# Rounding the next input over 75 slots, and another order of the weight jobs, in a one-core attention and gated-MLP kernel

## The chip, the cores and the metric

The kernel runs on one NeuronCore of a Trainium2 chip. The metric is the device time of one execution in microseconds (us). TensorE is PE in the rows (its weight loads PEld), VectorE is DVE, ScalarE is ACT, GpSimd is POOL, and SyncE (SP) issues the DMAs.

## The reference

One layer over x (4 batch elements of 512 rows by 512), with a second input ctx of the same size:

```python
x = x + tanh(g_xattn) * xattn(layernorm(x), ctx)
x = x + tanh(g_ffn) * ffn(layernorm(x))
```

xattn normalises its input and rounds it to fp8 (e4m3) four times, once for each of four projections, because q, qx, k and v each have an input scale of their own: q and qx of 16 heads of 128, k and v of 8 groups. kx and vx come from ctx without rounding. q attends over k and v, qx over kx and vx, and the two results (4096 columns) are rounded to fp8 and projected back to 512 columns. ffn is a gated MLP of width 2048 whose weights are ternary: every matrix is divided by the mean of its absolute values, rounded and cut to -1, 0 or 1:

```python
scale = jnp.clip(jnp.mean(jnp.abs(w)), EPS, None)
wq = jnp.clip(jnp.round(w / scale), -1.0, 1.0) * scale
```

The scale of a matrix has to be known before any part of it can be made ternary. That is the only order that the mathematics asks of the jobs below.

## The kernel before, in words

The program has two phases. Phase A does all attention, phase B the output projection and the MLP, 16 tiles of 128 rows. The change touches phase A only.

Phase A is a software pipeline of 512 **slots** (NSLOT). Each engine has a program of its own that runs `for n in range(FIRST, PAST)` and writes, slot by slot, what that engine does in it. Sixteen slots make one **iteration**: one batch element with one of the eight head groups, so iteration 0 to 7 is batch element 0, and so on to iteration 31. In each slot PE computes one 128x512 tile of scores (L687), DVE takes its row maximum (L977), ACT its exponential (L1323), DVE the reciprocal of the row sum (L982), ACT the high half of the scaled result (L1334), DVE the low half (`lo`, L987), SP transposes both by DMA (L441), and PE multiplies them with v nine slots after the scores (L699). `scores(n)` waits for `lo` of slot n-4. Around this the tiles of the next iteration's projections run on PE (L654, L661), with their statistics and norms on DVE and POOL, and the transposes of heads (L674) with their scaling on ACT (L1316) and their splitting into two fp16 halves on POOL (L1573, L1579). Nothing is scheduled at run time: which slot holds what is fixed by tables of slot numbers, `X_AT`, `JOB_AT`, `SCALE_AT`, `FLAG_AT`, `WG_AT` and others.

Two kinds of extra work ride in the slots, and both are moved by the change.

**The next input** (`X_AT`). In the 128 slots of batch element b, the input of b+1 is loaded, normalised, and transposed on PE through one PSUM bank in the slots 19, 24, 35 and 51 of the 128 (`turn`, one 128-column part `kt` each). ACT scales each part four times into `xqt`, once for each of the four input scales v (`x_turned`, L1244), two in the slot of the transpose and two in the next. DVE then rounds to e4m3 (`x_quant`): 8 parts of 1024 columns, each in 5 instructions (L916, L919, L921, L923, L925), so 40 instructions, one in each of the slots 62 to 101. The parts go by scale and then by half; part 2v+half. The projections of b+1 start at slot 105 of the 128 and wait for the parts of their scale (`xq_value`). This happens three times: iterations 3 to 6 (2, 16, 16 and 6 instructions), 11 to 14 and 19 to 22, in the same pattern. DVE also takes the four maxima of ctx (L840) in slots 70 to 76; POOL spreads the result (L1489, slot 83), PE makes it whole (`c_whole`, L606, slot 84).

**The weight jobs** (`JOBS`, 128 of them besides one marker called scale). A job loads 128x512 of a weight matrix into `raw[0]` or `raw[1]`, in turns:
- a *sum* (48) adds up absolute values on ACT (L1356; the read of its accumulator has a record of its own);
- a *split* (32, for the output weights) writes an fp16 half on ACT (L1348), subtracts it on POOL (L1603), takes absolute sums of the rest on ACT (L1364), and stores the rest;
- a *tern* (48) multiplies by 1/scale and adds the rounding constant on ACT (L1361), finishes on DVE (L1013, L1014), and is stored by DMA.

`job_slots` puts the jobs at every 8/3 slots: first sums and splits mixed, three sums and two splits in turn, in slots 92 to 302; then the scale; then the 48 terns in slots 309 to 437. The job of slot n has its load issued two jobs earlier, its ACT part in slot n (tern, split) or n+2 (sum, and a split's absolute sum), its DVE or POOL part in n+1, its store in n+3. `weight_sums` (DVE, slot 303), `scale_whole` (PE, L611, slot 308) and `weight_scales` (DVE, slot 309) turn the sums into the scales. `scale_whole` writes the same single PSUM bank that the head transposes and `turn` use (`ring_tables`, list `short`), and waits until its last user's readers are through. `low_sum` and `flag_whole` do the same for a flag on whether the low halves of the output weights are zero.

## Time and profile before

| | us |
|---|---|
| median of 3 runs | 1812.07 |
| the runs | 1807.82 to 1817.33 |
| profiled execution, its own time | 1815.84 |
| its span in the trace | 1814.1 |
| busy in the span: PE, DVE, ACT, POOL | 1620.1, 1533.6, 1371.8, 1100.2 |

Busy shares are averages over stages. The 512 slots lie between 114.8 us (first L977) and about 1489 us of the span; what is before is loading and preparing, what is behind is phase B. An iteration is read here as the time from every sixteenth L977 to the next, which is how the windows below were cut. A busy engine in the rows may include short waits inside a run of matmuls.

### The profile page before, as it was taken

The page shows a single profiled execution, that of the slowest core. Times are in us where ns is not written, and L with a number is a line of the kernel's source. Part 1 is how long each engine was busy: PE and PEld are TensorE (multiplying, and loading weights), DVE is VectorE, ACT ScalarE, POOL GpSimd, SP SyncE. Part 2 cuts the span into 40 slices and gives each one's busy share as a digit, 9 for nine tenths or more (in the row PEclk, how much of TensorE's full clock was granted, in tenths as well). Part 3 has the DMA queues.
Part 4 walks back from the last instruction along what each step waited for, and adds up shares of the span by engine and source line. Part 5 has one row for each costly group of instructions (what it writes and reads, how often), then busy time and mean ns, then how long its engine had stood idle before and what let it go on. Part 6 is the DMA issues. An engine that isn't in the chain of part 4 may idle for free.

```text
span 1814.1 us, 35237 instructions
## 1 busy us (share of the span) xinstructions
PE 1620.1 (89%) x11164; PEld 1005.9 (55%) x11164; DVE 1533.6 (85%) x3391; ACT 1371.8 (76%) x3439; POOL 1100.2 (61%) x1421
## 2 busy tenths in 40 slices
PE   2368899889999999999999898999999978999997
PEld 1345555555666665666566555666666633444443
DVE  7568889999897899989887999999988876777776
ACT  6458999879989998999998788899988872222222
POOL 3677888877887777787776666777767641000000
PEclk9689999999999999999999999999999999999999
DMA  3257888779999998999897989999998896243200
GB/s 104 90 151 164 186 194 190 178 169 230 230 244 196 218 226 191 205 217 250 193 216 169 224 192 200 222 229 225 251 222 169 184 246 216 70 112 87 76 24 18
DMA packets 669596, 325.48 MB, mean 179 GB/s; under 512 B 552288, under 2 KB 595424, under 8 KB 669152
## 3 DMA queue, kind: packets, MB, share of 16 engines
q1 hardware_dynamic: 669408, 323.17, 79.2%
q8 instruction: 93, 1.52, 0.4%
q14 instruction: 95, 0.78, 0.1%
HBM read 140.61 MB, written 48.23 MB: 104 GB/s over the span
## 4 chain that ended last, share of the span: by engine, by line
PE 45%; DVE 24%; ACT 12%; issue 8%; POOL 7%; DMA 4%; SPq 0%; ACTq 0%; POOLq 0%; DVEq 0%
PE psum L699 8%; PE psum L654 8%; PE psum L687 7%; PE psum L742 6%; PE psum L717 6%; DVE pp L987 5%; DVE nmx L977 5%; PE psum L661 3%; PE psum L760 3%; ACT pp L1334 2%; DMA pt<-pp 2%; ACT psum L1323 2%; PE psum L674 2%; ACT raw L1254 2%; DVE xh L960 1%
## 5 line engine op out<-in xcount | busy, mean ns | idle before, releaser
L687 PE MATMUL psum<-qk 128*128 128x512 f16 x1536 | 422.5, 384 | 21.6 <-DVE pp L987 15.8
L699 PE MATMUL psum<-pt,vv 128*128 128x512 f16 x1536 | 399.3, 383 | 37.2 <-ACT cy L1342 22.4
L654 PE MATMUL psum<-wbt,xqt 128*128 128x256 f16 (+1 forms) x4096 | 408.7, 249 | 22.1 <-DVE xqt L904 11.4
L1323 ACT ACTIVATE psum<-psum,nmx 128x512 f32<-128x512 f32 x512 | 352.4, 688 | 69.6 <-DVE nmx L977 68.0
L654 PEld LDWEIGHTS psum<-wbt,xqt 128*128 128x128 f16 x4096 | 329.5, 99 | 136.2 <-issue 18.4
L987 DVE SCALAR_TENSOR_TENSOR pp<-psum,prs,pp 128x512 f16<-128x512 f32 x512 | 378.7, 740 | 3.3 <-ACT pp L1334 3.3
L1334 ACT ACTIVATE pp<-psum,prs 128x512 f16<-128x512 f32 x512 | 366.0, 715 | 6.2 <-DMA pt<-pp 5.9
L977 DVE TENSOR_REDUCE nmx<-psum 128x1 f32<-128x512 f32 x512 | 344.8, 674 | 28.6 <-PE psum L687 28.0
L699 PEld LDWEIGHTS psum<-pt,vv 128*128 128x128 f16 x1536 | 147.5, 98 | 234.5 <-issue 54.2
L1579 POOL TENSOR_TENSOR qk<-y,qk 128x512 f16<-128x512 f32 x192 | 231.8, 1207 | 16.0
L687 PEld LDWEIGHTS psum<-qk 128*128 128x128 f16 x1536 | 143.8, 99 | 105.4 <-DVE pp L987 24.8
L661 PE MATMUL psum<-wbt,ctxh 128*128 128x256 f16 x1536 | 193.3, 277 | 0.3 <-POOL wbt L1531 0.3
L661 PEld LDWEIGHTS psum<-wbt,ctxh 128*128 128x128 f16 x1536 | 152.5, 99 | 47.2 <-issue 2.2
L1316 ACT ACTIVATE y<-psum,hb,hw 128x512 f32<-128x512 f32 x192 | 156.7, 816 | 9.4 <-PE psum L674 9.2
L1591 POOL TENSOR_TENSOR cy<-cy,cc 128x512 f16<-128x512 bf16 x128 | 152.2, 1190 | 13.1 <-DVE cy L1001 13.1
L1329 ACT ACTIVATE prs<-psm 128x1 f32<-128x1 f32 x512 | 120.0, 234 | 51.9 <-DVE psm L982 51.3
L1664 POOL TENSOR_SCALAR frs<-fmv 128x1 f32<-128x1 f32 x16 | 3.1, 193 | 255.6 <-DVE fmv L1043 255.5
L1554 POOL TENSOR_TENSOR ars<-ast,eps 128x4 f32<-128x4 f32 x128 | 36.1, 282 | 186.1 <-DVE ast L947 185.7
L1557 POOL TENSOR_TENSOR ars<-ars,mhalf 128x4 f32<-128x4 f32 x128 | 133.7, 1044 | 10.0
L1573 POOL TENSOR_SCALAR qk<-y 128x512 f16<-128x512 f32 x192 | 120.8, 629 | 30.1 <-ACT y L1316 22.4
L1448 ACT ACTIVATE sl<-psum,am 128x512 f32<-128x512 f32 x64 | 44.0, 688 | 124.5 <-PE psum L742 124.5
L982 DVE RECIPROCAL psm<-psm 128x1 f32<-128x1 f32 x512 | 78.7, 154 | 68.1 <-ACT psum L1323 66.7
(176 smaller groups left out, 2792.3 us busy)
## 6 DMA issues: line engine op xcount, KB each, us to landing
wbt<-ws SPq DMA_DIRECT2D x192, 256.0 KB, 3.7
ws<-wbt SPq DMA_DIRECT2D x64, 256.0 KB, 4.1
catd<-cy SPq DMA_DIRECT2D x64, 256.0 KB, 3.2
raw<-in_wgu SPq DMA_DIRECT2D x64, 256.0 KB, 3.6
raw<-in_w SPq DMA_DIRECT2D x32, 384.0 KB, 3.9
wbt<-catd SPq DMA_DIRECT2D x6, 2048.0 KB, 9.8
pt<-pp SPq DMA_TRANSPOSE x512, 3.8
raw<-in_wp SPq DMA_DIRECT2D x32, 256.0 KB, 3.6
```

What stands on the lines that cost most here:

```text
L654: ins = e.matmul(bank[:, o0:o0 + c1 - c0], xv[:, v, kt * 512 + tt * 128:kt * 512 + (tt + 1) * 128], wb[i][:, h, kt, c0:c1], start=kt == 0 ...
L661: ins = e.matmul(bank[:, 256:512], ctxh[:, u, kt, ts], wkvb[i][:, w, kt, :], start=kt == 0 and k == 0, stop=kt == 3 and k == 2)
L687: ins = e.matmul(SB(n), qk[i][:, jq, u, ss], qk[i][:, jk, w, :], start=k == 0, stop=k == 2)
L699: ins = e.matmul(OB, v[:, t, u, att, :], src[:, w, t, :], start=t == 0 and k == 0, stop=t == 3 and k == 2)
L977: e.tensor_reduce(nmx[:, n % 8:n % 8 + 1], SB(n), AX, ALU.max, negate=True).then_inc(s["mx"], 1)
L987: e.scalar_tensor_tensor(pp[k][:, 1, :], SB(n), prs[:, n % 8:n % 8 + 1], pp[k][:, 0, :], ALU.mult, ALU.subtract).then_inc(s["lo"], 1)
L1316: e.activation(y32[n % 2][:], psum[:, BANK["T", n], :], ACT.Identity, bias=hb[:, vec:vec + 1], scale=hw[:, vec:vec + 1]).then_inc(s["y32"], 1)
L1323: e.activation(SB(n), SB(n), ACT.Exp, bias=nmx[:, k], accum_out=psm[:, k]).then_inc(s["exp"], 1)
L1334: e.activation(pp[n % 4][:, 0, :], SB(n), ACT.Copy, scale=prs[:, n % 8:n % 8 + 1]).then_inc(s["hi"], 1)
L1557: e.tensor_tensor(rs[:, 1, :], rs[:, 0, :], mhalf[:, 0:4], ALU.pow).then_inc(s["a_rs"], 1)
L1579: e.tensor_tensor(qk[it % 2][:, j, 1, :], y32[n % 2][:], qk[it % 2][:, j, 0, :], ALU.subtract).then_inc(s["hd_lo"], 1)
L1591: e.tensor_tensor(y.bitcast(F16), y, tmp, ALU.subtract).then_inc(s["o_q"], 1)
```

## The change

- `X_AT["quant"]`: the 40 rounding instructions lie in the slots 28 to 102 of the 128, at 28 + 1.9k, so 75 slots, about every second one. Parts are ordered by half first and scale second, so the first four parts need only the transposes of slots 19 and 24 (`xy_value(b, 2 * half_ + 1, v)`). `xq_value` is adapted to the new order: the last part of scale v is number 4+v.
- `JOBS` is ordered: all 48 sums and 8 splits (slots 92 to 230), the scale (232), 20 terns (236 to 285), 24 splits with 4 terns among them (288 to 359), 24 terns (362 to 438). With the new rounding slots (28 to 102, 156 to 230, 284 to 358) the first 20 terns lie between the second and the third rounding, and all but 8 splits lie in the third.
- `SCALE_AT` moves from 303, 308 and 309 to 218, 228 and 229; `FLAG_AT` from 306, 324 and 325 to 366, 372 and 373; `WG_AT` from 444 to 448.
- The waits for an earlier store or absolute sum of the same buffer are left out where there was none (`stored`, `summed` is None).

Counted by iteration, before and after:

| iteration | 1 | 2 | 3 | 4 | 5 | 6 | 9 | 10 | 11 | 12 | 13 | 14 | 15 | 16 | 17 | 18 | 19 | 20 | 21 | 22 | 23-27 |
|---|---|---|---|---|---|---|---|---|---|---|---|---|---|---|---|---|---|---|---|---|---|
| rounding before | 0 | 0 | 2 | 16 | 16 | 6 | 0 | 0 | 2 | 16 | 16 | 6 | 0 | 0 | 0 | 0 | 2 | 16 | 16 | 6 | 0 |
| rounding after | 3 | 8 | 8 | 9 | 8 | 4 | 3 | 8 | 8 | 9 | 8 | 4 | 0 | 0 | 3 | 8 | 8 | 9 | 8 | 4 | 0 |
| terns before | | | | | | | 0 | 0 | 0 | 0 | 0 | 0 | 0 | 0 | 0 | 0 | 4 | 6 | 6 | 6 | 26 |
| terns after | | | | | | | 0 | 0 | 0 | 0 | 0 | 2 | 6 | 6 | 6 | 1 | 0 | 1 | 1 | 3 | 22 |
| splits before | | | | | | 2 | 2 | 2 | 2 | 3 | 3 | 2 | 2 | 2 | 3 | 3 | 0 | 0 | 0 | 0 | 0 |
| splits after | | | | | | 0 | 0 | 0 | 0 | 0 | 6 | 2 | 0 | 0 | 0 | 6 | 6 | 5 | 5 | 2 | 0 |

```diff
--- before.py
+++ after.py
@@ -44,12 +44,12 @@
 STORE_W = 10
 POOL_HI = 2
 ACT_NORM = 2 * 4
-WG_AT, CAT_AT, X2_AT = (444, 490), (474, 498), 507
+WG_AT, CAT_AT, X2_AT = (448, 490), (474, 498), 507
 RAMP = -4
 OUT_AT = {"clip": 17, "field": 18, "step": 19, "add": 20, "sub": (21, 23), "store": 26}
-JOBS_FROM, TERN_FROM = 92, 309
-SCALE_AT = {"sum": 303, "whole": 308, "fac": 309}
-FLAG_AT = {"sum": 306, "whole": 324, "fac": 325}
+JOBS_FROM = 92
+SCALE_AT = {"sum": 218, "whole": 228, "fac": 229}
+FLAG_AT = {"sum": 366, "whole": 372, "fac": 373}
 X_AT = {
     "load": (1, 2, 3, 4),
     "stats": (6, 8, 9, 10),
@@ -57,7 +57,7 @@
     "norm": (13, 14, 15, 16),
     "turn": (19, 24, 35, 51),
     "ctx": (62, 63, 64, 65),
-    "quant": tuple(range(62, 102)),
+    "quant": tuple(28 + k * 19 // 10 for k in range(40)),
     "bound": (70, 72, 74, 76),
     "cxp": (82,),
     "cxs": (83,),
@@ -143,9 +143,11 @@
 
 SUMS = [("sum", "wgu", j, j) for j in range(32)] + [("sum", "wd", j, 32 + j) for j in range(16)]
 SPLITS = [("split", "wp", j, j) for j in range(32)]
-JOBS = [t for i in range(16) for t in SUMS[3 * i:3 * i + 3] + SPLITS[2 * i:2 * i + 2]]
-JOBS += [("scale", None, 0, 0)]
-JOBS += [("tern", "wgu", j, j) for j in range(32)] + [("tern", "wd", j, 32 + j) for j in range(16)]
+TERNS = [("tern", "wgu", j, j) for j in range(32)] + [("tern", "wd", j, 32 + j) for j in range(16)]
+JOBS = SUMS + SPLITS[:8] + [("scale", None, 0, 0)] + TERNS[:20]
+JOBS += [t for i in range(4) for t in SPLITS[8 + 6 * i:14 + 6 * i] + TERNS[20 + i:21 + i]] + TERNS[24:]
+
+JOB_SPANS = ((92, 231, 56), (232, 233, 1), (236, 288, 20), (288, 362, 28), (362, 442, 24))
 K0 = 6 * NG
 LAST_SPLIT = max(m for m, job in enumerate(JOBS) if job[0] == "split")
 LAST_SUM = max(m for m, job in enumerate(JOBS) if job[0] == "sum")
@@ -153,9 +155,10 @@
 
 def job_slots():
 
-    scale = JOBS.index(("scale", None, 0, 0))
-    at = {JOBS_FROM + m * 8 // 3: m for m in range(scale)}
-    at.update({TERN_FROM + (m - scale) * 8 // 3: m for m in range(scale, len(JOBS))})
+    at, m = {}, 0
+    for first, last, count in JOB_SPANS:
+        at.update({first + k * (last - first) // count: m + k for k in range(count)})
+        m += count
     at[JOBS_FROM - 4] = -1
     return at
 
@@ -240,7 +243,7 @@
 
 
 def xq_value(b, v):
-    return v + 1 if b == 0 else 4 + 8 * (b - 1) + 2 * v + 2
+    return v + 1 if b == 0 else 4 + 8 * (b - 1) + 4 + v + 1
 
 
 class Queue:
@@ -906,11 +909,11 @@
             def x_quant(b, k):
 
                 part, step = divmod(k, 5)
-                v, half_ = divmod(part, 2)
+                half_, v = divmod(part, 4)
                 src = xq[b % 2][:, v, half_ * 1024:(half_ + 1) * 1024]
                 tmp, done = xtmp[:], s["x_w"]
                 if step == 0:
-                    q.wait_ge("xy", xy_value(b, 3, v))
+                    q.wait_ge("xy", xy_value(b, 2 * half_ + 1, v))
                 q.wait_ge("x_w", ((b - 1) * 8 + part) * 4 + step)
                 if step == 0:
                     e.tensor_scalar(src, src, 448.0, -448.0, ALU.min, ALU.max).then_inc(done, 1)
@@ -1008,8 +1011,10 @@
                 f, ob = raw[i][:, 0:512], raw[i][:, 512:768].bitcast(BF16)[:, 0:512]
                 stored, summed = JB[m]
                 q.wait_ge("l_t1", JV["l_t1", m])
-                q.wait_ge(f"l_st{i}", JV[f"l_st{i}", stored])
-                q.wait_ge("l_ab", JV["l_ab", summed])
+                if stored is not None:
+                    q.wait_ge(f"l_st{i}", JV[f"l_st{i}", stored])
+                if summed is not None:
+                    q.wait_ge("l_ab", JV["l_ab", summed])
                 q.done(e.tensor_scalar(ob, f, MAGIC, 1.0, ALU.subtract, ALU.min))
                 e.tensor_scalar(ob, ob, -1.0, None, ALU.max).then_inc(s["l_t2"], 1)
 
@@ -1599,6 +1604,7 @@
                     q.wait_ge("l_hi", JV["l_hi", m])
                     if stored is not None:
                         q.wait_ge(f"l_st{i}", JV[f"l_st{i}", stored])
+                    if summed is not None:
                         q.wait_ge("l_ab", JV["l_ab", summed])
                     e.tensor_tensor(o.bitcast(F16)[:, 0:512], f, wps[:, j, :], ALU.subtract).then_inc(s["l_lo"], 1)
 
```

What the engines' programs are then: first DVE in slots 328 and 329 (iteration 20). Before (L977 is the row maximum that opens a slot, L987 `lo`, L916 and L919 rounding, L840 ctx, L1013 and L1014 a tern):

```order
L977 TENSOR_REDUCE nmx<-psum 128x1
L987 SCALAR_TENSOR_TENSOR pp2<-psum,prs,pp2 128x512
L954 BN_STATS bst1<-psum 128x6
L916 TENSOR_SCALAR xqt<-xqt 128x1024
L840 TENSOR_REDUCE cpt<-xt 128x1
L1013 TENSOR_SCALAR raw1<-raw1 128x512
L1014 TENSOR_SCALAR raw1<-raw1 128x512
L982 RECIPROCAL psm<-psm 128x1
L977 TENSOR_REDUCE nmx<-psum 128x1
L987 SCALAR_TENSOR_TENSOR pp3<-psum,prs,pp3 128x512
L937 SCALAR_TENSOR_TENSOR vv0<-psum,vv0 128x256
L919 TENSOR_SCALAR xtmp<-xqt 128x1024
```

And in the changed kernel, the same two slots whole (its line numbers are three higher from L843 on: L980 for L977, L928 for L925, which is a rounding instruction):

```order
L980 TENSOR_REDUCE nmx<-psum 128x1
L990 SCALAR_TENSOR_TENSOR pp2<-psum,prs,pp2 128x512
L957 BN_STATS bst1<-psum 128x6
L843 TENSOR_REDUCE cpt<-xt 128x1
L985 RECIPROCAL psm<-psm 128x1
L980 TENSOR_REDUCE nmx<-psum 128x1
L990 SCALAR_TENSOR_TENSOR pp3<-psum,prs,pp3 128x512
L940 SCALAR_TENSOR_TENSOR vv0<-psum,vv0 128x256
L928 TENSOR_TENSOR xqt<-xqt,xtmp 128x1024
L985 RECIPROCAL psm<-psm 128x1
```

In slot 328 three instructions are gone (one of rounding, two of a tern); slot 329 keeps one of rounding.

ACT in slots 329 and 330. Before (L1323 exponential, L1334 high half, L1361 a tern's part):

```order
L1323 ACTIVATE psum,psm<-psum,nmx 128x512
L1334 ACTIVATE pp0<-psum,prs 128x512
L1307 ACTIVATE xh1<-psum,brs1 128x128
L1308 ACTIVATE xh1<-psum,brs1 128x128
L1329 ACTIVATE prs<-psm 128x1
L1323 ACTIVATE psum,psm<-psum,nmx 128x512
L1334 ACTIVATE pp1<-psum,prs 128x512
L1316 ACTIVATE y32_0<-psum,hb,hw 128x512
L1361 ACTIVATE raw0<-raw0,magic,wsc 128x512
L1329 ACTIVATE prs<-psm 128x1
```

In the changed kernel (L1328 exponential, L1339 high half, L1353 and L1369 the two ACT parts of splits):

```order
L1328 ACTIVATE psum,psm<-psum,nmx 128x512
L1339 ACTIVATE pp0<-psum,prs 128x512
L1312 ACTIVATE xh1<-psum,brs1 128x128
L1313 ACTIVATE xh1<-psum,brs1 128x128
L1369 ACTIVATE raw0,lsum<-raw0 128x512
L1334 ACTIVATE prs<-psm 128x1
L1328 ACTIVATE psum,psm<-psum,nmx 128x512
L1339 ACTIVATE pp1<-psum,prs 128x512
L1321 ACTIVATE y32_0<-psum,hb,hw 128x512
L1353 ACTIVATE wps<-raw1 128x512
L1334 ACTIVATE prs<-psm 128x1
```

The tern's one instruction is replaced by a split's two, of two different splits here.

PE in slots 307 and 308. Before (L626 is the transpose of the next input, L611 `scale_whole`):

```order
L687 MATMUL psum<-qk1 128x512 x3
L699 MATMUL psum<-pt0,vv0 128x512 x3
L654 MATMUL psum<-wbt,xqt 128x128 x16
L626 MATMUL psum<-idf,xt 128x128 x4
L687 MATMUL psum<-qk1 128x512 x3
L661 MATMUL psum<-wbt,ctxh 128x256 x12
L611 MATMUL psum<-wsc,ones 128x2
```

In the changed kernel (L629 the transpose, L690 scores):

```order
L690 MATMUL psum<-qk1 128x512 x3
L702 MATMUL psum<-pt0,vv0 128x512 x3
L657 MATMUL psum<-wbt,xqt 128x128 x16
L629 MATMUL psum<-idf,xt 128x128 x4
L690 MATMUL psum<-qk1 128x512 x3
L664 MATMUL psum<-wbt,ctxh 128x256 x12
```

The `scale_whole` directly behind the transpose of the next input is gone from here; it stands in slot 228, which is not behind such a transpose.

## Rows read from the trace of the kernel before

**Rows 1.** The page: busy time by engine; the row maximum's group, busy us, mean ns.

```profile
PE 1620.1 (89%) x11164; PEld 1005.9 (55%) x11164; DVE 1533.6 (85%) x3391; ACT 1371.8 (76%) x3439; POOL 1100.2 (61%) x1421
...
L977 DVE TENSOR_REDUCE nmx<-psum 128x1 f32<-128x512 f32 x512 | 344.8, 674 | 28.6 <-PE psum L687 28.0
```

**Rows 2.** Windows: stretch, its us, busy us (instructions) by engine, PEclk, DMA share, GB/s.

```profile
214.90:311.80 96.90, 85.94 (x612) 56.23 (x613) 86.80 (x189) 91.71 (x243) 84.27 (x104) 0.96 0.86 190
311.80:413.40 101.60, 84.00 (x590) 53.25 (x588) 97.47 (x211) 83.45 (x221) 82.03 (x96) 0.95 0.79 186
...
537.20:578.20 41.00, 37.96 (x285) 25.22 (x284) 33.31 (x76) 40.55 (x108) 30.23 (x41) 1.00 0.89 190
578.20:659.30 81.10, 79.59 (x603) 53.88 (x602) 66.47 (x151) 77.28 (x210) 60.67 (x81) 1.00 1.02 216
659.30:748.60 89.30, 83.86 (x612) 54.80 (x610) 87.37 (x192) 77.56 (x206) 67.33 (x83) 0.98 0.99 215
...
790.20:828.40 38.20, 38.20 (x290) 25.68 (x289) 32.87 (x76) 35.69 (x101) 30.28 (x41) 1.00 1.08 232
828.40:871.00 42.60, 42.56 (x322) 28.71 (x320) 38.09 (x87) 37.38 (x102) 34.54 (x49) 1.00 1.10 241
871.00:914.70 43.70, 39.23 (x282) 25.73 (x280) 34.20 (x76) 41.26 (x108) 29.34 (x40) 0.96 0.84 191
914.70:954.50 39.80, 39.80 (x303) 26.98 (x302) 33.57 (x78) 39.22 (x106) 31.25 (x42) 1.00 1.05 219
954.50:1002.30 47.80, 44.63 (x319) 29.66 (x317) 38.20 (x87) 38.70 (x98) 30.77 (x41) 0.93 0.81 176
1002.30:1099.80 97.50, 85.35 (x602) 53.97 (x600) 95.03 (x216) 76.68 (x188) 62.19 (x78) 0.96 0.94 203
1099.80:1144.00 44.20, 39.22 (x288) 24.86 (x287) 43.99 (x97) 37.89 (x96) 31.59 (x40) 1.00 0.86 199
...
1183.70:1304.00 120.30, 118.29 (x890) 79.01 (x888) 116.86 (x259) 108.50 (x277) 87.19 (x115) 1.00 1.08 230
1342.60:1420.90 78.30, 78.30 (x594) 53.10 (x593) 66.03 (x149) 66.64 (x173) 56.00 (x77) 1.00 0.96 198
```

**Rows 3.** Timeline of PE: start, us, instruction, and in brackets its idle time before.

```profile
380.62 0.77 PE L606 MATMUL psum<-spread,ones 128*128 128x128 f32 x2 [6.66 <-POOL spread L1489]
...
969.32 0.59 PE L611 MATMUL psum<-wsc,ones 128*128 128x2 f32 x2 [3.17 <-ACT xqt L1244]
...
1016.62 1.39 PE L699 MATMUL psum<-pt,vv 128*128 128x512 f16 x3 [3.71 <-DMA pt<-pp]
...
1064.20 0.50 PE L606 MATMUL psum<-spread,ones 128*128 128x128 f32 x2 [2.74 <-POOL spread L1489]
```

**Rows 4.** A rounding group of DVE in 659.3 to 748.6 us: busy us, mean ns.

```profile
L919 DVE TENSOR_SCALAR xtmp<-xqt 128x1024 uint16<-128x1024 uint16 x7 | 6.0, 861 | 0.0
```

**Rows 5.** The tern's DVE groups in 1002.3 to 1099.8 us.

```profile
L1013 DVE TENSOR_SCALAR raw<-raw 128x512 bf16<-128x512 f32 x12 | 6.0, 503 | 0.0
...
L1014 DVE TENSOR_SCALAR raw<-raw 128x512 bf16<-128x512 bf16 x12 | 3.5, 294 | 0.4
```

**Rows 6.** The job groups of ACT, and POOL's, over the whole span.

```profile
L1361 ACT ACTIVATE raw<-raw,magic,wsc 128x512 f32<-128x512 f32 x48 | 40.6, 845 | 2.4 <-DMA raw<-in_wgu 1.3 <-DMA raw<-in_wd 1.1
L1603 POOL TENSOR_TENSOR raw<-raw,wps 128x512 f16<-128x512 f32 x32 | 38.6, 1206 | 3.0 <-ACT wps L1348 3.0
L1356 ACT ACTIVATE raw<-raw 128x512 f32<-128x512 f32 x48 | 32.3, 673 | 0.0
L1348 ACT ACTIVATE wps<-raw 128x512 f16<-128x512 f32 x32 | 21.7, 679 | 0.7 <-DMA raw<-in_wp 0.7
L1364 ACT ACTIVATE raw<-raw 128x512 f32<-128x512 f16 x32 | 21.4, 669 | 7.7 <-POOL raw L1603 7.7
```

**Rows 7.** Timeline at 714 us: a GpSimd and a VectorE instruction.

```profile
713.98 1.20 POOL L1579 TENSOR_TENSOR qk<-y,qk 128x512 f16<-128x512 f32 x1
714.10 1.36 DVE L919 TENSOR_SCALAR xtmp<-xqt 128x1024 uint16<-128x1024 uint16 x1
```

## The prediction

> **What bounds the kernel now.** The page gives PE 89%, DVE 85%, ACT 76% of the span [rows 1]. Such an average settles nothing for a change that only moves work, so I read the windows by iteration [rows 2]: which engine is full, and where. Four kinds of stretch show.
>
> - Iterations 28 and 29 (1342.6 to 1420.9) have no rounding and no job: 39.15 us each, PE busy all of it, DVE 33.0, ACT 33.3. That is the floor, set by PE. Iterations 24 to 26 add 18 terns: DVE goes to 38.95 each (97%), and the time only to 40.1.
> - Iterations 12 and 13 (659.3 to 748.6) hold 32 rounding instructions: DVE 87.4 of 89.3 us, 98%. Iterations 20 and 21 (1002.3 to 1099.8) hold as many and 12 terns: DVE 95.0 of 97.5. Iteration 22 has DVE 44.0 of 44.2. DVE sets the pace there; PE's `scores` wait for `lo`, which DVE gives late.
> - Iteration 9 (537.2 to 578.2) has ACT 40.55 of 41.0; iteration 17 ACT 41.3 of 43.7. Two transposes of the next input fall into each, eight scalings on ACT, beside mixed jobs.
> - Iterations 2 and 3 (214.9 to 311.8) have ACT 91.7 of 96.9, DVE 86.8; iterations 4 and 5 (311.8 to 413.4) DVE 97.5 of 101.6.
>
> The rounding is thus bunched in three places where DVE is full, with PE-bound iterations that leave DVE 6 us each on both sides. The timeline of PE [rows 3] shows single stalls in the same places: 6.66 and 2.74 us before `c_whole` in iterations 5 and 21, whose chain starts on the late DVE, and 3.17 us before `scale_whole` in iteration 19, where PE waits for ACT to read the transpose that lies in the same bank. The granted clock of iteration 19 is 0.93 of full [rows 2]: it fell from 2.4 to 1.2 GHz for part of the stretch, after that idle time. So a stall is paid twice.
>
> **Prices.** *Rounding instruction on DVE.* Iterations 12 and 13 have 87.37 - 2 x 33.02 = 21.3 us more than the floor [rows 2]; 2.7 us I give to the four ctx maxima, at the 0.674 us of the row maximum, a reduction of the same size [rows 1]. The rest by 32 is 0.58 us, which I take. Ends: 0.4, if nothing holds it up, and 0.86, the mean of one of the five steps there [rows 4].
> *Tern on DVE.* Where DVE is full, 0.503 + 0.294 = 0.80 us [rows 5]; in iterations 24 to 26 (116.86 - 3 x 33.02)/18 = 0.99 [rows 2]. I take 0.8 where one is removed from a full DVE, 0.9 where one is added.
> *A job on ACT.* By mean durations [rows 6] a tern is 0.85, a sum 0.67, a split 0.68 + 0.67 = 1.35 (and an accumulator read with sum and split, of some 0.24). Records of ACT overlap, so busy time grows by less: a tern adds (108.5/3 - 33.3)/6 = 0.47 us. Bounds are therefore 0.5 and 1 of the durations.
> *Time over the fullest engine.* Where DVE is full the iteration takes 1.0 to 1.2 us more than DVE's busy time (44.65 over 43.7; 48.75 over 47.5). I use 1.0.
>
> **The change part by part**, by iteration, against the rows.
>
> 1. *Second rounding, iterations 9 to 14.* The jobs beside it become sums. Iteration 9: ACT loses two splits for three sums, and DVE gets 3 instructions at 0.58, under cover of ACT and PE: -0.6. Iterations 10 and 11: DVE 33.2 + 8 x 0.58 = 37.9, under PE's 39.8 of 40.55: 0. If this cover fails, each costs what the terns cost in 24 to 26, 0.95. Iterations 12 and 13: 15 instructions fewer, -8.7 on DVE, to 39.3 each; now PE sets the pace, as in 10 and 11 (81.1 for two). I take 82.0 for 89.3: -7.3. Iteration 14: two instructions less, two terns more: 0. Sum **-7.9**.
> 2. *Twenty terns in iterations 14 to 18.* Iteration 15 becomes like 24 to 26: 38.2 to 40.1, +1.9. Iteration 16 has DVE 38.1 already (loading and norms of x): + 6 x 0.9 = 43.5, DVE-bound, 44.5 for 42.6: +1.9. Iteration 17: DVE 34.2 + 5.4 + 3 x 0.58 = 41.3, so 42.3 for 43.7, since ACT has terns in place of splits: -1.4. Sum **+2.4**. Price if DVE waits for GpSimd more: below.
> 3. *Third rounding with splits, iterations 18 to 22.* Iteration 18: DVE 33.6 + 8 x 0.58 + 0.9 = 39.1. On ACT, 6 splits, a tern and four scalings come to less than the two scalings-of-four plus six jobs of iteration 9, which ran in 41.0: 41.3 for 39.8, +1.5. Iteration 19: the same load, and `scale_whole` with its 3.17 us stall and the clock's fall are gone, also four terns: 41.5 for 47.8, -6.3. Iterations 20 and 21: DVE 95.0 - 15 x 0.58 - 10 x 0.8 = 78.3, 39.2 each; ACT takes ten splits for ten terns; I take 41.2 each, 82.4 for 97.5: -15.1. This includes the stall before `c_whole`, which should shrink with a DVE on time. Iteration 22: DVE 44.0 - 2 x 0.58 - 3 x 0.8 = 40.4, so 41.4: -2.8. Sum **-22.7**.
> 4. *First rounding, iterations 1 to 6.* Iterations 1 to 3 get 17 instructions while ACT is fullest there (91.7 of 96.9): +2, twice the price of six terns. Iterations 4 and 5 lose 15, -8.7 on DVE; but ACT and GpSimd are at 83 and 82 of 101.6 and near the next bound, so I take -6 of it. Sum **-4.0**.
> 5. *The rest.* Iterations 23 to 27 have four terns fewer at 0.95/6 = 0.16: **-0.6**. `weight_sums`, `weight_scales`, the flag: the same few instructions elsewhere, in slots where no transpose of x is directly ahead in the bank; 0. `WG_AT` four slots later: loads that are used in phase B, tens of slots on; 0. SP issues the same transfers; terns' stores now fall in iterations 15 to 18 with DMA shares of 0.84 to 1.10, where 24 to 26 ran at 1.08 with them. If SP's queue were late, the transposes (`pt`) would be, and PE with them. Phase B and the head of the program are untouched.
>
> Sum: -7.9 + 2.4 - 22.7 - 4.0 - 0.6 = -32.8. The profiled execution took 1815.84 us, so **1783 us**, 1.8% less. It lies 3.8 us above the median of the runs, a difference I leave inside the range.
>
> **A rule against the change.** At 714 us a rounding instruction (L919) that can take 0.4 us takes 1.36, and ends 0.28 us after a GpSimd instruction that began just before it and took 1.20 [rows 7]. The Trainium skill, "SBUF — State Buffer", section "Who interferes with whom", says that such instructions of the two engines share one pair of ports and that the one that starts later waits for the whole of the other. By that rule the splits are the wrong company for the rounding: each brings a GpSimd instruction that reads SBUF; what that gives at worst is rival (a).
>
> **The rivals.**
> (a) *GpSimd holds up the rounding.* 24 splits bring 24 subtractions of 1.21 us [rows 6] into iterations 18 to 22; in 20 to 22 the rounding had none before. At worst each delays DVE by all of it: 5.8 us per iteration, DVE 45 and the iteration 46, so +22 and 1805. For it: the row at 714 us, and L919's mean of 0.86 in iterations 12 and 13 [rows 4], which had splits. Against: half the slots hold no rounding, and GpSimd is busy only 31.25 of 39.8 us in iteration 18 [rows 2]. Half of it is more likely: 1794. A full ACT there gives the same. Chance of about half or more: 0.18.
> (b) *More is gained*: the spread work is hidden in PE's time altogether, the stalls of iterations 4 to 5 and 12 to 13 vanish with their clock losses, and iterations 15 and 18 stay at their times: 10 to 12 us less, 1772. Chance 0.10.
> (c) *It moves and does not go*: what leaves the bunches returns in the iterations that were PE-bound, because DVE has no slack at the moment `lo` is needed. 24 to 26 speak against it, at 97% and 40.1. About 1808: chance 0.06.
> (d) *Slower*: a rounding or tern instruction ahead of `lo` in every second slot makes each of iterations 9 to 22 as slow as 12 and 13 were, 44.65 us. 14 x 44.65 = 625 for the 607 that they take now: +18, and with nothing gained earlier 1834. It turns to a loss, these iterations alone, from 43.3 us each. Chance 0.04.
> That the change would not do what it says can be left out: the order of instructions shows the rounding thinned and the terns gone from iterations 20 and 21.
>
> **How the numbers follow.** My forecast (1776 to 1793) has 0.62, (a) 0.18, (b) 0.10, (c) 0.06, (d) 0.04. The range 1767 to 1802 takes in forecast, (b) and most of (a). A measurement of this kernel can tell about 0.5%, 9 us, from no change: faster (below 1803) 0.90, same 0.06, slower 0.04.
>
> **What would show it.** Iterations 12 and 13 at 41 us each with DVE near 39; 19 to 21 at 41 to 42, no idle PE before the scale's matmul, granted clock 1.0; 15 and 16 slower by 2 each; 24 to 29 unchanged. Wrong would be: iterations 18 to 21 above 44 with DVE or ACT above 97%, or rounding instructions with a mean above 0.8 us there.

## The result, and the profile after

The changed kernel takes 1798.99 us (median of 6 runs, 1795.99 to 1801.12); the kernel before took 1814.07 in 6 runs on the same chip. The ratio is 0.9918, with a 95% interval of 0.9902 to 0.9935. It is faster, by 15.1 us or 0.8%. The forecast was 1783.0 with a range of 1767 to 1802: the time is in the range, the gain is less than half of the forecast one (32.8). The profiled execution took 1801.12 us, its span is 1798.7, so 15.4 less than the 1814.1 of before.

The page of the changed kernel, busy time by engine, and the row maximum's group (L980 now, busy us, mean ns, idle before):

```profile
PE 1618.2 (90%) x11164; PEld 1004.5 (56%) x11164; DVE 1542.9 (86%) x3391; ACT 1372.2 (76%) x3439; POOL 1103.8 (61%) x1421
...
L980 DVE TENSOR_REDUCE nmx<-psum 128x1 f32<-128x512 f32 x512 | 345.2, 674 | 19.2 <-PE psum L690 18.3
```

The same work in the same number of instructions as in [rows 1]; DVE's busy time is 9.3 us longer, though nothing was added: the 120 rounding instructions, by count and mean duration of their five groups, sum to 77.4 us before and 85.4 after.

Windows of the changed kernel, cut as in [rows 2] at every sixteenth row maximum: iterations 2 to 3 and 4 to 5, then 9, 10 to 11, 12 to 13, 14, 15, 16, 17, 18, 19, 20 to 21 and 22, then 24 to 26 and 28 to 29. The columns are those of [rows 2]:

```profile
216.20:314.60 98.40, 84.90 (x607) 54.42 (x605) 93.36 (x202) 91.31 (x242) 87.41 (x104) 0.98 0.85 185
314.60:413.40 98.80, 84.09 (x589) 53.36 (x587) 89.97 (x197) 83.56 (x223) 79.68 (x97) 0.93 0.79 188
534.80:576.20 41.40, 39.06 (x295) 26.13 (x294) 35.38 (x80) 40.27 (x106) 28.80 (x39) 1.00 0.92 197
576.20:655.40 79.20, 79.20 (x600) 53.55 (x598) 76.55 (x166) 75.56 (x205) 57.25 (x76) 1.00 1.01 215
655.40:738.50 83.10, 80.57 (x606) 54.00 (x604) 79.62 (x178) 76.25 (x205) 64.62 (x82) 1.00 1.02 227
738.50:782.80 44.30, 40.84 (x301) 26.35 (x300) 40.88 (x88) 41.04 (x106) 36.83 (x46) 1.00 0.94 201
782.80:822.10 39.30, 38.61 (x292) 25.84 (x292) 37.40 (x89) 36.23 (x92) 28.17 (x39) 1.00 1.05 225
822.10:866.60 44.50, 41.24 (x302) 26.46 (x300) 42.85 (x99) 37.37 (x92) 32.65 (x46) 1.00 1.14 248
866.60:911.60 45.00, 41.26 (x298) 27.32 (x299) 40.43 (x92) 41.70 (x100) 28.97 (x39) 0.96 0.85 197
911.60:954.70 43.10, 40.72 (x306) 27.09 (x305) 39.47 (x84) 40.13 (x106) 35.33 (x43) 1.00 0.92 212
954.70:996.70 42.00, 39.65 (x295) 25.90 (x293) 38.71 (x86) 40.22 (x106) 34.81 (x43) 1.00 1.00 221
996.70:1086.20 89.50, 82.14 (x605) 53.26 (x603) 81.54 (x180) 79.26 (x210) 72.24 (x90) 1.00 0.98 218
1086.20:1129.10 42.90, 39.12 (x290) 25.33 (x289) 41.25 (x89) 39.90 (x104) 35.23 (x44) 1.00 0.87 210
1169.40:1287.80 118.40, 116.79 (x881) 78.36 (x879) 112.88 (x252) 105.78 (x272) 83.80 (x114) 1.00 1.02 224
1326.20:1404.40 78.20, 78.20 (x594) 53.02 (x592) 65.86 (x148) 66.40 (x173) 55.87 (x77) 1.00 0.98 199
```

Read against [rows 2], in us, and beside the prediction's terms:

| iterations | before | after | change | forecast |
|---|---|---|---|---|
| start of the span to 1 | 165.3 | 166.3 | +1.0 | 0 |
| 1 to 3 | 146.5 | 148.3 | +1.8 | +2 |
| 4, 5 | 101.6 | 98.8 | -2.8 | -6 |
| 6 to 8 | 123.8 | 121.4 | -2.4 | 0 |
| 9 to 11 | 122.1 | 120.6 | -1.5 | -0.6 |
| 12, 13 | 89.3 | 83.1 | -6.2 | -7.3 |
| 14 | 41.6 | 44.3 | +2.7 | 0 |
| 15, 16 | 80.8 | 83.8 | +3.0 | +3.8 |
| 17 | 43.7 | 45.0 | +1.3 | -1.4 |
| 18 | 39.8 | 43.1 | +3.3 | +1.5 |
| 19 | 47.8 | 42.0 | -5.8 | -6.3 |
| 20, 21 | 97.5 | 89.5 | -8.0 | -15.1 |
| 22 | 44.2 | 42.9 | -1.3 | -2.8 |
| 23 to 27 | 198.6 | 197.1 | -1.5 | -0.6 |
| 28 to the end | 471.5 | 472.5 | +1.0 | 0 |
| all | 1814.1 | 1798.7 | -15.4 | -32.8 |

Where a change was forecast its sign is right except in 17, but 17.4 us are missing: 7.1 in iterations 20 and 21, 3.2 in 4 and 5, and 8.7 in 14, 17, 18 and 22 together, with small differences of both signs elsewhere. The place to look is 18 to 22. There no engine is full now: in 20 and 21 PE is busy 82.1 of 89.5 us (92%), DVE 81.5 (91%), ACT 79.3 (89%), POOL 72.2 (81%), where DVE had 95.0 of 97.5 before. Yet the two iterations take 11 us more than the floor of 78.2.

The view of waits says between whom. The changed kernel, iterations 18 to 22 (911.6 to 1129.1); engine, line, what it waited for: us in total, times, longest:

```profile
DVE psm L985 <- ACT psum L1328: 9.9, 14, 1.5
PE psum L702 <- ACT cy L1347: 8.0, 10, 1.2
...
DVE cc L1000 <- POOL cy L1590: 5.9, 6, 1.6
```

Of the kernel before, over 914.7 to 1144.0:

```profile
DVE psm L982 <- ACT psum L1323: 4.4, 8, 1.2
...
PE psum L699 <- ACT cy L1342: 4.2, 7, 0.9
```

Two waits grew to twice their size, and one is new: DVE's step on the attention output (L1000) waits for GpSimd's clip (L1590), 5.9 us where there was no such wait. The chain of waits agrees: the work that ended last in a window, followed back from its end. Changed kernel, iterations 20 and 21 (996.7 to 1086.2), shares by engine and line:

```profile
by line: issue 12.5%; POOL raw L1609 8.9%; POOL qk L1584 8.1%; POOL cy L1596 7.2%; DVE nmx L980 6.7%; DVE pp L990 6.6%; POOL qk L1578 5.2%; POOL cy L1590 3.5%; POOL ars L1562 3.4%; ACT pp L1339 2.8%; POOL brs L1572 2.7%; DVE xqt L919 2.6%; 
```

In the kernel before the largest shares of the chain of iterations 20 and 21 were DVE's `pp` (17.1%) and `nmx` (13.0%), and none of its twelve largest was POOL's. Now POOL's lines above make up 39% of it, and the largest of a line is L1609, the subtraction of a split. (Over all of 18 to 22 L1609 has 5.8%, behind `pp` with 8.7% and `nmx` with 8.6%.) The timeline of the changed kernel shows one case; start, us, instruction, idle before:

```profile
1001.33 1.16 POOL L1609 TENSOR_TENSOR raw<-raw,wps 128x512 f16<-128x512 f32 x1
...
1002.45 0.62 POOL L1578 TENSOR_SCALAR qk<-y 128x512 f16<-128x512 f32 x1
...
1003.16 1.16 POOL L1584 TENSOR_TENSOR qk<-y,qk 128x512 f16<-128x512 f32 x1
...
1004.40 1.04 POOL L1590 TENSOR_SCALAR cy<-cy 128x1024 bf16<-128x1024 bf16 x1
...
1005.47 0.43 DVE L1000 TENSOR_SCALAR cc<-cy 128x1024 uint16<-128x1024 uint16 x1 [1.60 <-POOL cy L1590]
...
1006.23 0.67 DVE L980 TENSOR_REDUCE nmx<-psum 128x1 f32<-128x512 f32 x1
...
1006.82 0.74 DVE L990 SCALAR_TENSOR_TENSOR pp<-psum,prs,pp 128x512 f16<-128x512 f32 x1
...
1006.93 0.66 ACT L1328 ACTIVATE psum<-psum,nmx 128x512 f32<-128x512 f32 x1 [0.39 <-DVE nmx L980]
...
1007.61 0.33 PEld L690 LDWEIGHTS psum<-qk 128*128 128x128 f16 x3 [0.77 <-DVE pp L990]
```

GpSimd works with gaps of at most 0.09 us: subtraction, head split (two instructions), clip. The clip ends at 1005.44; DVE stood idle for 1.60 us before it took up L1000. Behind L1000, in DVE's own order, are the next row maximum and `lo`, so ACT (0.39 us) and PE (0.77 us) wait for them in turn. That is the theory I took to the chip (**G**): what a split costs is that its 1.16 us sit in GpSimd's queue ahead of the clip. The rivals: **A**, it is ACT, whose split has two instructions and two places in its queue; **S**, neither job in particular: a slot that already carries more than it can is late, whatever the average, so it matters in which slots the rounding lies. And rival (a) of the prediction: the subtraction makes DVE's own instructions longer.

### The profile page after: what moved, and what is told of

The parts are those of the page before. It is cut to its first block, busy times and chain, and to the rows that moved or that the text cites. A ratio compares the mean times of both kernels' runs of the same rounds, so it can differ in the third digit from the quotient of the medians.

```text
span 1798.7 us, 35237 instructions
## 1 busy us (share of the span) xinstructions
PE 1618.2 (90%) x11164; PEld 1004.5 (56%) x11164; DVE 1542.9 (86%) x3391; ACT 1372.2 (76%) x3439; POOL 1103.8 (61%) x1421
## 3 DMA queue, kind: packets, MB, share of 16 engines
q1 hardware_dynamic: 669408, 323.17, 79.3%
## 4 chain that ended last, share of the span: by engine, by line
PE 42%; DVE 24%; ACT 13%; POOL 10%; issue 8%; DMA 3%; SPq 0%; ACTq 0%; POOLq 0%; DVEq 0%
PE psum L702 7%; PE psum L657 7%; PE psum L690 6%; PE psum L745 6%; PE psum L720 6%; DVE pp L990 5%; DVE nmx L980 5%; PE psum L664 3%; PE psum L763 3%; ACT pp L1339 2%; ACT psum L1328 2%; DMA pt<-pp 2%; ACT raw L1259 2%; PE psum L677 2%; DVE xh L963 1%
## 5 line engine op out<-in xcount | busy, mean ns | idle before, releaser
L690 PE MATMUL psum<-qk 128*128 128x512 f16 x1536 | 422.1, 384 | 20.3 <-DVE pp L990 14.4
L1328 ACT ACTIVATE psum<-psum,nmx 128x512 f32<-128x512 f32 x512 | 349.4, 682 | 67.3 <-DVE nmx L980 66.0
L1339 ACT ACTIVATE pp<-psum,prs 128x512 f16<-128x512 f32 x512 | 362.7, 708 | 4.4 <-DMA pt<-pp 4.3
L980 DVE TENSOR_REDUCE nmx<-psum 128x1 f32<-128x512 f32 x512 | 345.2, 674 | 19.2 <-PE psum L690 18.3
L1584 POOL TENSOR_TENSOR qk<-y,qk 128x512 f16<-128x512 f32 x192 | 234.6, 1222 | 16.0
L690 PEld LDWEIGHTS psum<-qk 128*128 128x128 f16 x1536 | 143.7, 99 | 103.5 <-DVE pp L990 21.7
L1334 ACT ACTIVATE prs<-psm 128x1 f32<-128x1 f32 x512 | 117.2, 229 | 44.0 <-DVE psm L985 43.0
L1578 POOL TENSOR_SCALAR qk<-y 128x512 f16<-128x512 f32 x192 | 121.4, 632 | 28.9 <-ACT y L1321 22.4
L745 PE MATMUL psum<-xqt,h1t 128*128 128x512 bf16 x512 | 119.3, 386 | 3.6 <-ACT h1t L1447 1.8
```

Source lines behind the costliest of these rows:

```text
L690: ins = e.matmul(SB(n), qk[i][:, jq, u, ss], qk[i][:, jk, w, :], start=k == 0, stop=k == 2)
L745: ins = e.matmul(dst, h1t[T % 2][:, kt, :], wgs[:, kt, c0:c0 + 512], start=kt == 0, stop=kt == 3)
L980: e.tensor_reduce(nmx[:, n % 8:n % 8 + 1], SB(n), AX, ALU.max, negate=True).then_inc(s["mx"], 1)
L1328: e.activation(SB(n), SB(n), ACT.Exp, bias=nmx[:, k], accum_out=psm[:, k]).then_inc(s["exp"], 1)
L1339: e.activation(pp[n % 4][:, 0, :], SB(n), ACT.Copy, scale=prs[:, n % 8:n % 8 + 1]).then_inc(s["hi"], 1)
L1584: e.tensor_tensor(qk[it % 2][:, j, 1, :], y32[n % 2][:], qk[it % 2][:, j, 0, :], ALU.subtract).then_inc(s["hd_lo"], 1)
```

## The experiments

**Rounding alone.** The kernel before with the new rounding slots and the new order of parts; jobs and scale as before. (Of the diff only the slots; the order of parts is changed as in the change.)

```diff
-    "quant": tuple(range(62, 102)),
+    "quant": tuple(28 + k * 19 // 10 for k in range(40)),
```

> The kernel before with the change's rounding (75 slots, halves first) alone; jobs, scale and flag stay where they were. Theory G (in the changed kernel GpSimd's queue, with six splits an iteration, sets the pace of iterations 18 to 22): here the splits stay thin (2 or 3 an iteration) and the terns share iterations 20 to 22 with only half as many rounding instructions, so 20 and 21 take about 44 us each (before 48.8), 12 and 13 about 41.5, 19 stays at 47 to 48 with its stall at the scale. Total 1815 - 19 = 1796, as good as the whole change. Rival C of the prediction (work moved out of the bunches returns elsewhere): 1808 to 1814. Theory A (ACT's share of the splits sets the pace): the same as G here.

Measured: 1806.23 us, 0.9958 of before (0.9941 to 0.9974), 10 us above what was expected. In 20 and 21, where the terns stay, DVE is still full: 88.8 of 91.9 us.

**Jobs alone.** The change with the old rounding slots (the diff the other way round).

> The changed kernel with the rounding back in slots 62 to 101. Iterations 12 and 13 return to 44 to 45 us each (+5 in all), 4 and 5 to 101 (+3). Theory G: iterations 20 and 21 have 32 rounding instructions and ten splits, DVE 95 - 8 = 87 of about 93 us, so 46 each; 15 to 18 keep their loss of about 7, 19 its gain of 6. Total 1808 to 1812. If the order of jobs carried the gain, it would stay near 1800.

Measured: 1813.24 us, 0.9996 (0.9983 to 1.0009), just above what was expected. Windows, rounding alone, iterations 12 to 13 and 20 to 21:

```profile
660.30:743.50 83.20, 80.06 (x603) 53.78 (x601) 78.79 (x175) 76.93 (x206) 65.25 (x83) 1.00 1.06 221
...
996.70:1088.60 91.90, 83.69 (x598) 54.18 (x597) 88.81 (x200) 75.78 (x188) 61.29 (x78) 0.96 0.96 210
```

Jobs alone, 12 to 13, 14 to 17, and 20 to 21:

```profile
657.10:747.90 90.80, 83.33 (x612) 53.72 (x609) 89.33 (x192) 77.48 (x204) 67.15 (x82) 1.00 0.94 206
...
747.90:918.80 170.90, 158.43 (x1178) 104.41 (x1179) 161.71 (x361) 155.14 (x389) 125.82 (x166) 1.00 0.98 217
...
1002.80:1095.60 92.80, 82.96 (x607) 53.01 (x604) 88.85 (x196) 79.86 (x209) 73.41 (x89) 1.00 1.00 213
```

The gain of 12 and 13 is the rounding's (89.3 to 83.2): these two take 80.9 to 85.2 us in all eleven runs with spread rounding and 86.5 to 90.8 in the three without. In 20 and 21 each part takes some 5 us (97.5 to 91.9 and to 92.8), both together 8. The new order of jobs is worth nothing by itself: its gains in 19 (6.1 us) and 20 to 21 (4.7) are paid back in 14 to 17, 170.9 us for 166.1, and in 18 (+2.5) and 12 to 13 (+1.5). By the medians the parts give 8 and 1 and both together 15; by the profiled spans 10.9, 3.6 and 15.4. So whether they help each other is not settled: the medians say so, the spans don't.

**Theory G: a short subtraction.** The changed kernel, with GpSimd's subtraction cut to 32 of 512 columns. Two more lines follow from it: the absolute sum on ACT reads these 32 columns 16 times (mean 0.677 us for 0.670), and the store takes the high half in place of the rest. The low half is not computed.

```diff
-                    e.dma_start(wpld[:, j], raw[i][:, 512:768].bitcast(F16)).then_inc(s[f"l_st{i}"], 16)
+                    e.dma_start(wpld[:, j], wps[:, j, :]).then_inc(s[f"l_st{i}"], 16)
...
-                    e.activation(f, o.bitcast(F16)[:, 0:512], ACT.Abs, accum_out=lsum[:, j:j + 1]).then_inc(s["l_ab"], 1)
+                    e.activation(f.rearrange("p (a b) -> p a b", b=32), o.bitcast(F16)[:, 0:32].unsqueeze(1).broadcast_to([128, 16, 32]), ACT.Abs,
+                                 accum_out=lsum[:, j:j + 1]).then_inc(s["l_ab"], 1)
...
-                    e.tensor_tensor(o.bitcast(F16)[:, 0:512], f, wps[:, j, :], ALU.subtract).then_inc(s["l_lo"], 1)
+                    e.tensor_tensor(o.bitcast(F16)[:, 0:32], f[:, 0:32], wps[:, j, 0:32], ALU.subtract).then_inc(s["l_lo"], 1)
```

> The changed kernel; GpSimd's subtraction of a split covers 32 of 512 columns (about 0.2 us instead of 1.16). The rest of the low half is not computed: the absolute sum on ACT reads those 32 columns 16 times, so it keeps its size, and the store writes the high half in its place. Theory G: iterations 18 to 22 lose most of what they have over 41.5 us: from 217.5 to about 208, and 13 and 14 one or two us; total 1799 - 10 = 1789. Theory A (ACT): 0 to -2. Theory P (the shared ports lengthen the rounding): the mean of the five rounding groups falls from about 0.69 to about 0.55 us, 40 instructions, -3 at most to -5.

Measured: 1790.61 us, 0.9876 (0.9857 to 0.9895), so 8.4 us less than the change. Its waits in iterations 18 to 22:

```profile
DVE psm L985 <- ACT psum L1328: 9.6, 15, 1.1
...
PE psum L702 <- ACT cy L1347: 4.0, 7, 0.9
...
DVE cc L1000 <- POOL cy L1591: 0.2, 1, 0.2
```

and its windows of 18 to 22 and of 20 to 21:

```profile
989.20:1077.00 87.80, 82.98 (x611) 54.98 (x609) 81.87 (x181) 78.89 (x210) 62.77 (x89) 0.98 1.04 228
...
909.00:1119.80 210.80, 200.29 (x1482) 132.37 (x1482) 197.65 (x433) 198.07 (x523) 156.20 (x217) 0.99 1.03 224
```

The wait for the clip goes from 5.9 to 0.2 us, PE's wait for ACT's copy (L1347) from 8.0 to 4.0, and the five iterations from 217.5 to 210.8. That the subtraction costs, and about as much as G said, is shown. It does not explain all: iterations 20 and 21 stay at 87.8, and DVE's wait for ACT stays at 9.6. Nor is all of the gain shown to be the queue's. Of the 6.7 us only 1.7 are in 20 and 21, where the wait for the clip was 4.0 us; 4.9 are in 18 and 19 (85.1 to 80.2), where DVE's busy time fell by 3.6 us with the time. And a wait's sum is not its price: the short absolute sum of the next run takes PE's wait for L1347 to 4.6 as well, for 1.3 us.

The same run bears on rival (a) of the prediction, the shared ports. DVE's rounding groups in iterations 18 to 22, of the change:

```profile
L926 DVE TENSOR_TENSOR xqt<-xqt,xtmp 128x1024 bf16<-128x1024 bf16 x8 | 7.0, 874 | 0.0
L928 DVE TENSOR_TENSOR xqt<-xqt,xtmp 128x1024 f16<-128x1024 bf16 x8 | 6.9, 862 | 0.0
...
L919 DVE TENSOR_SCALAR xqt<-xqt 128x1024 bf16<-128x1024 bf16 x7 | 4.8, 681 | 0.0
...
L922 DVE TENSOR_SCALAR xtmp<-xqt 128x1024 uint16<-128x1024 uint16 x7 | 3.3, 473 | 0.0
```

and with the short subtraction:

```profile
L928 DVE TENSOR_TENSOR xqt<-xqt,xtmp 128x1024 f16<-128x1024 bf16 x8 | 8.1, 1009 | 0.0
...
L926 DVE TENSOR_TENSOR xqt<-xqt,xtmp 128x1024 bf16<-128x1024 bf16 x8 | 6.2, 773 | 0.0
...
L922 DVE TENSOR_SCALAR xtmp<-xqt 128x1024 uint16<-128x1024 uint16 x7 | 3.7, 535 | 0.0
L919 DVE TENSOR_SCALAR xqt<-xqt 128x1024 bf16<-128x1024 bf16 x7 | 3.5, 495 | 0.0
```

Single steps are longer in one and shorter in the other. With the fifth step (L924: 0.583 us times 7 and 0.655 times 8) the mean of all is 26.1/37 = 0.71 us in the change and 26.7/38 = 0.70 with the short subtraction. Long subtractions do not lengthen the rounding as a whole. The run with the rounding alone agrees: in 20 and 21, where no split lies, its rounding instructions have a mean of 0.72 us, as the change's have there (0.73).

One by one, though, DVE instructions are held up, by splits too. Changed kernel, iteration 20:

```profile
1031.20 1.34 POOL L1609 TENSOR_TENSOR raw<-raw,wps 128x512 f16<-128x512 f32 x1
1031.45 1.37 DVE L919 TENSOR_SCALAR xqt<-xqt 128x1024 bf16<-128x1024 bf16 x1
```

L919 takes 0.41 us at its shortest in 18 to 22; here it ends 0.28 us after the subtraction. Of all DVE instructions of 18 to 22 that are over 0.08 us longer than the shortest of their line, five stand behind a split's subtraction so, with 2.6 us more than their shortest in all, and thirteen behind the second part of the head split (L1584), with 9.5 us. With the short subtraction none stands behind it, and ten, with 8.1 us, behind the head split. So rival (a) acts, but on five instructions and not on all 24; it is part of the fall of DVE's busy time in 18 to 22 (201.0 to 197.7).

**Theory A: a short absolute sum.** The changed kernel, ACT's second part of a split on 32 columns.

```diff
-                    e.activation(f, o.bitcast(F16)[:, 0:512], ACT.Abs, accum_out=lsum[:, j:j + 1]).then_inc(s["l_ab"], 1)
+                    e.activation(f[:, 0:32], o.bitcast(F16)[:, 0:32], ACT.Abs, accum_out=lsum[:, j:j + 1]).then_inc(s["l_ab"], 1)
```

> The changed kernel; the absolute sum of a split on ACT covers 32 of 512 columns (the flag then looks at those alone). ACT gets back 0.4 us a split, 2.4 us in each of iterations 18 and 19. Theory A: iterations 18 to 22 fall by 2 each, total 1790. Theory G: 0 to -3, 1796 to 1799.

Measured: 1797.16 us, 0.9901 (0.9885 to 0.9918). ACT's busy time in 18 to 22 falls from 199.5 to 191.5, the time from 217.5 to 216.2. DVE's wait for ACT falls from 9.9 to 5.2. A is out as the main cause: 8 us of relief on ACT are worth 1.3, though half of that wait is gone.

**The stall before the scale, by itself.** The kernel before with `SCALE_AT` at 301, 304 and 305 for 303, 308 and 309.

> The kernel before; only the sums' reduction, the scale's matmul and its factors go from slots 303, 308, 309 to 301, 304, 305, ahead of the transpose of slot 307. If the stall of 3.17 us and the clock's fall behind it explain iteration 19, that falls from 47.8 to about 43.5 and the total to 1810 or 1811. If iteration 19 only paid for load that is there anyway, it stays at 47 to 48 and the total at 1814.

Measured: 1809.55 us, 0.9984 (0.9971 to 0.9997). Iteration 19 takes 43.3 us for 47.8, 20 and 21 together 95.3 for 97.5. So 4.5 of the 5.8 us that the change gains in iteration 19 come from these three instructions, the matmul among them, which no longer lies behind the transpose of the next input in its bank: its stall is 1.61 us for 3.17, the clock of the iteration 1.00 for 0.93. That was independent of the order of the jobs. The run also shows how single iterations scatter: up to slot 301 its program is that of the kernel before, and yet iteration 9 takes 42.7 us for 41.1, 12 and 13 take 86.5 for 89.3.

**Theory G used: the splits moved away.** Eight splits instead of 24 beside the third rounding, 24 behind the last terns, in slots 438 to 500.

```diff
+JOBS = SUMS + [("scale", None, 0, 0)] + TERNS[:20] + SPLITS[:8] + TERNS[20:] + SPLITS[8:]
+JOB_SPANS = ((92, 214, 48), (232, 233, 1), (236, 288, 20), (290, 358, 8), (362, 437, 28), (438, 500, 24))
```

Here and in the later runs with another order the diff is cut: the flag's instructions move behind the last split (slots 503 to 506), and the load of the ternary weights waits for the last two terns by name.

> The changed kernel with the splits in other slots: 48 sums in 92 to 211, 20 terns as now, 8 splits thin in 290 to 350, 28 terns in 362 to 434, 24 splits in 438 to 497, where no rounding, no ctx work and no tern is; flag in 503 to 506; the load of the ternary weights waits for the last terns. Theory G (splits crowd GpSimd beside rounding): iterations 18 to 22 fall from 217.5 to 206 to 209, as with the small subtraction and better; 27 to 30 rise by 1 to 4 in all. Total 1799 - 8 = 1790, range 1786 to 1794. If a split costs the same everywhere (0.8 us or so each), nothing is gained: 1797 to 1801.

Measured: 1798.13 us, 0.9918 (0.9890 to 0.9947), no gain over the change where 1790 was expected. Its windows of 18 to 22, 23 to 26 and 27 to 30:

```profile
905.80:1110.00 204.20, 198.94 (x1490) 132.54 (x1489) 196.51 (x425) 181.69 (x472) 157.21 (x201) 1.00 0.93 193
...
1110.00:1273.90 163.90, 159.99 (x1186) 104.33 (x1185) 161.67 (x346) 144.75 (x369) 115.11 (x153) 1.00 1.02 223
1273.90:1435.20 161.30, 151.17 (x1099) 98.07 (x1097) 132.35 (x294) 151.58 (x410) 132.85 (x166) 1.00 1.09 241
```

Where the splits left, the time left too: 204.2 for 217.5. But 23 to 26 have six terns each and take 163.9 for 158.7, and 27 to 30, which were almost free of jobs, take 161.3 for 152.0. There DVE is at 82%, and the splits still cost 0.4 us each. What 18 to 22 gained, 13.3 us, these two stretches gave back (14.5).

**Theory S: lighter slots.** The changed kernel, rounding kept out of the slots with n mod 8 = 2 or 3, in which DVE has the output's steps.

```diff
+    "quant": tuple([n for n in range(28, 103) if n % 8 not in (2, 3)][k * 56 // 40] for k in range(40)),
```

> The changed kernel with the rounding kept out of the slots whose number by 8 leaves 2 or 3, where DVE already has the field and step of the output rounding and the norm (a slot of 3.4 to 4.4 us against 2.2 for a light one). Theory S (the slot, not the iteration, is what has to fit: `lo` may be only four slots late, so a heavy slot is not paid back by a light one): iterations 2, 18 to 22 lose 1 to 2 us each, total 1799 - 6 = 1793. If averages over an iteration decide, no change, 1797 to 1801.

Measured: 1794.10 us, 0.9897 (0.9875 to 0.9918), some 5 us less than the change: the same instructions over the same 75 slots. By the intervals of the whole time alone the two kernels can't be told apart. Iterations 18 to 22 take 213.3 for 217.5, and that comes again in the two later pairs that differ in this: 204.2 to 199.8 with late splits, 210.7 to 205.4 with the mixed order. So in which slots the rounding lies is a second cause. Why it is one is not shown. DVE's busy time falls by about as much as the time in each pair (3.8, 5.2 and 5.4 us), in the first mostly in the rounding, whose mean falls from 0.70 to 0.63 us (2.7 us of the 3.8), so fewer hold-ups by GpSimd fit it as well as S, the slots that carry too much. The wait for the clip stays at 5.2.

**Both** (late splits, lighter slots):

> Both of the last two. If the two effects are separate they add: 1784 (G and S both right), 1790 (G alone), 1793 (S alone). Iterations 18 to 22 at 40.5 to 41.5 each.

Measured: 1793.91 us, 0.9885 (0.9860 to 0.9911). 18 to 22 are at 199.8, which is 39.96 an iteration, 0.8 above the floor, but the price of the late splits remains, and in the whole time the two do not add (1784 was expected if they did).

**A mixed order.** Half as many splits beside the third rounding (12 and 4 terns), 16 behind the terns.

```diff
+JOB_SPANS = ((92, 222, 52), (232, 233, 1), (236, 288, 20), (288, 362, 16), (362, 442, 24), (443, 503, 16))
```

> The changed kernel with the splits thin everywhere: 4 behind the sums, 12 (with 4 terns) over slots 288 to 358 where 24 were, 16 alone in slots 443 to 500, and the terns where the change has them. Theory G: iterations 18 to 22 fall from 217.5 to 205 to 208 (204 was measured with 8 splits there), 13 falls by 2, 27 to 31 rise by about 5 in all (10 was measured with 24 splits). Total 1799 - 8 = 1791, range 1787 to 1795. If the number of splits is what costs and not their density: 1797 or more.

Measured: 1796.52 us, 0.9907 (0.9879 to 0.9936), a miss: 18 to 22 at 210.7 where 205 to 208 were expected, 27 to 30 at 153.7 for 152.0.

**The bank of `c_whole`.** The changed kernel with it one slot later, since PE stood 6.6 us before it in iteration 5 and 1.97 in iteration 21.

```diff
-    "cxw": (84,),
-    "cxf": (85,),
+    "cxw": (85,),
+    "cxf": (86,),
```

> The changed kernel with `c_whole` on PE and the factor on DVE one slot later (85 and 86). The stall ahead of it (6.62 us in iteration 5, 1.58 and 1.97 in 13 and 21) loses up to a slot, 2 to 3 us, in iteration 5, and the clock there stays up longer: iteration 5 falls from 49.2 to 45 to 46.5, 13 and 21 by 0 to 1.5. Total 1799 - 4 = 1795. If GpSimd, late by itself, sets the pace of iteration 5 (38 of 49 us busy), the wait moves elsewhere: 1798 to 1800.

Measured: 1803.74 us, 0.9947 (0.9930 to 0.9964), slower than the change by 5. Timeline of PE in the change, and then here:

```profile
1054.53 0.46 PE L609 MATMUL psum<-spread,ones 128*128 128x128 f32 x2 [1.97 <-POOL spread L1494]
```

```profile
1063.90 1.11 PE L677 MATMUL psum<-idf,xh 128*128 128x128 f32 x4 [3.93 <-DVE cfa L838]
```

The stall did not go, it moved to the next user of the bank and doubled: the head transposes now wait for DVE to read `c_whole`'s result, which stands late in DVE's order. Iteration 21 takes 47.9 us for 43.7, its clock is at 0.93 for 1.00. In iteration 5 the stall of 6.62 us is down to 0.38, with one of 2.32 before the head transposes, and the iteration gains 1.0; but it takes 48.0 and 48.1 also in the runs with the short subtraction and with lighter slots, which keep 6.6 and 6.5 us of stall, so that gain is not shown to come from the stall.

**All three** (mixed order, lighter slots, later `c_whole`), and last **without the later `c_whole`**:

> g1, g3 and the rounding in light slots together. Additive: 1791 - 4 - 4 = 1783, range 1780 to 1791. It should beat both the kernel before and the changed one.

> g4_mix_all without its moved c_whole (which stays in slot 84 of the 128): the mixed order of the jobs and the rounding kept out of slots 2 and 3 of eight. In g3_cwhole the moved c_whole cost 1.7, 2.1 and 4.3 us in iterations 9, 13 and 21 and gave 1.0 and 1.3 in 5 and 24, because the stall of 1.97 us before it became one of 3.93 us before the head transposes that follow it in the bank. If that is so here too, this kernel takes 2 to 5 us less than g4_mix_all: 1785 to 1788 us, iteration 21 below 43.5. If the price belongs to g3 alone, 1790 as g4_mix_all.

Measured: 1789.81 us, 0.9880 (0.9848 to 0.9913), where the sum of the three was 1783, and 1788.41, 0.9864 (0.9841 to 0.9887). The last is the fastest of all runs, 10 us below the change and 27 below the kernel before. Its windows of 18 to 22 and 20 to 21:

```profile
903.70:1109.10 205.40, 198.82 (x1488) 132.19 (x1487) 195.13 (x433) 187.11 (x489) 165.65 (x206) 1.00 0.97 208
...
983.90:1068.20 84.30, 80.51 (x602) 53.35 (x601) 80.55 (x181) 73.13 (x193) 66.69 (x83) 1.00 0.96 206
```

Iteration 21 took 42.4 us where the one with the later `c_whole` took 44.3, as expected from the run before. (Iteration 9, which that expectation also names, holds no `c_whole`; its 41.2 for 42.7 is within the scatter seen above.) The difference of the two in whole, 1.4 us, is less than the intervals can tell.

## Why the prediction was half right

**What held.** The bunched rounding was the bound of 12 and 13: 83.1 us for the 82.0 taken, with DVE at 79.6 (39.8 each for the 39.3 worked out). The scale's stall and its clock loss went: iteration 19 at 42.0 for 41.5, clock 1.00. Terns beside PE-bound work cost 3.0 in 15 and 16 for 3.8. The rounding did cost little in 10 and 11: 79.2. The rounding instructions had a mean of 0.70 us in 18 to 22, below the 0.8 of the text, though two of the five steps were above it (0.874 and 0.862).

**What failed, first: the time over the fullest engine.** This is the term of the sum that was too small, and with it the wait that part 3 did not have. I priced an iteration as its fullest engine's busy time plus 1 us (in part 3, for 20 and 21, plus 2 each). That figure came from stretches where DVE was at 97% or more and so hardly waited. With DVE at 91% the waits between the engines show: 20 and 21 take 8.0 us more than DVE's busy time, against the 82.4 - 78.3 = 4.1 that part 3 allowed. That is 3.9 of the missing 7.1 us. The waits name GpSimd's clip behind the split's subtraction (5.9 us in 18 to 22, 4.0 of them in 20 and 21). Taking the subtraction away removed that wait and gave 8.4 us over the whole kernel, about half of the 17.4 that are missing, but only 1.7 of the 3.9 in 20 and 21, where another 2.54 us of PE's time went into a late transposing DMA. Part 3 counted the split on ACT, and the prediction named GpSimd only as a partner on a port (rival (a)), never as a queue that DVE waits for. The instruction was in [rows 6] with its 1.206 us; the step left out was "what stands behind it, and who waits for that".

**Second: a term too small.** DVE's busy time in 20 and 21 came to 81.5, not 78.3: the other 3.2 us. The terns went as priced (8.1 us by their durations, for 8.0). The 15 rounding instructions fewer gave 7.5 us and not 8.7, because the 17 that stay are longer: 0.73 us, where the mean in the same stretch was 0.62 before. That is 1.2 of the 3.2; the other 2.0 no row names. The splits are not needed for that: the run with the rounding alone has 0.72 there. The price of 0.58 was busy time of iterations 12 and 13; by durations the mean there was 0.68. The sign that I had named for being wrong, iterations above 44 us with DVE or ACT above 97%, would have missed this: 20 and 21 took 44.75 on average at 91%.

**Third: iterations 17 and 14.** For 17 I took 1.4 us off because terns replace splits; it grew by 1.3, with ACT's busy time at 41.70 for 41.26. PE's stall before the head transposes, for ACT's scalings, stays (2.17 to 2.26 us). But that stall does not explain it: with the jobs alone iteration 17 has the same stall of 2.26 us and takes 42.2, as forecast, and with the rounding alone 42.8. Only both together take 45.0; why is open. In 14, two splits and two terns beside six sums and the last rounding gave +2.7 for 0. The run with the jobs alone has +4.7 there, so it is the jobs; which of them was not tried apart. The scale's matmul, which lies in 14 now, is not it: the stall behind it is 0.17 us.

**Iterations 4 and 5.** -2.8 for -6: the stall before `c_whole` stayed at 6.6 us (6.66 before [rows 3]), with a clock of 0.93 over the two. I had expected a DVE on time to shorten it. It did so in 21 (2.74 to 1.97) and not in 5. That the stall is what the missing 3.2 us went into is not shown: with it down to 0.38 (later `c_whole`) iteration 5 gained 1.0.

**The rivals.** By its number (a), 1794 to 1805, was nearest and had 0.18. The culprit it named was right. The way it named, by the port, occurs but is small: five DVE instructions in 18 to 22 with 2.6 us, where the rival had up to 1.21 us for each of 24, and the rounding as a whole has 0.71 us with long subtractions and 0.70 without. The wait for the clip, by order, is the other way. The short subtraction takes both away at once, so their shares of the 8.4 us are not separated. That (a)'s number was near is in part luck: it priced one of the two ways, at more than it measured. (d) did not occur. (c) did not in the main, since 12, 13, 20 and 21 did fall, though 14, 17 and 18 grew by 2.7, 1.3 and 3.3 us.

**What stays open.** Even with a short subtraction, 20 and 21 take 87.8 us, with 9.6 us of DVE waiting for ACT's exponentials in 18 to 22. One piece is a transposing DMA that comes 2.5 us late at one place; the rest is many waits under 1.2 us. That it matters which slots hold the rounding is shown in three pairs of runs (4 to 5 us in 18 to 22), but no run separates full slots from the shorter rounding instructions that came with them. And why 24 splits in iterations with DVE at 82% still cost 9 us is not explained.

## What to carry to other kernels

When a change takes work off the fullest engine, price the rest by the waits between the engines and not by the next busy share: for every instruction that is moved onto an in-order queue, ask which instruction stands behind it and who waits for that one, and which instructions of its port partner will start while it runs. Then take it away in a test: the sum of a wait in the profile is not its price. Try other slots for spread work before other amounts; the same instructions over the same 75 slots differed by 4 to 5 us. And look first at lone stalls that share a buffer or a bank: one matmul moved by four slots, with its two companions, was worth 4.5 us of its iteration, but another moved by one slot handed its stall to the next user of the bank, doubled in iteration 21.

## What the runs showed of the hardware

DVE instructions that start while a GpSimd subtraction is under way end behind it: L919 at 1031.45 us took 1.37 us for 0.41 and ended 0.28 us after L1609; seven of the ten L1002 of 18 to 22 took 0.93 to 1.33 us for 0.41 and ended 0.27 to 0.29 us after L1584. With the short subtraction the output's two steps behind the clip were shorter: 0.423 for 0.518 us (L1000) and 0.828 for 0.916 (L1002), ten of each in 18 to 22, 1.8 us in all. The Trainium skill, "SBUF — State Buffer", section "Who interferes with whom", says that the later of two such instructions waits for the whole of the earlier one; for single instructions the trace agrees. But few of them meet: at every one of the 24 subtractions of 1.23 us such a wait would sum to 30 us; five DVE instructions waited so, with 2.6 us, and DVE's busy time in these iterations differs by 3.3 us between the two kernels (201.0 and 197.7).

A single stall of PE can have a price beyond its length. Behind the stall of 3.93 us before the head transposes (later `c_whole`) the granted clock is 0.50, the lower of its two levels, 1.2 GHz for 2.4:

```profile
1064.00:1067.00 3.00, 3.00 (x10) 1.54 (x11) 0.67 (x2) 0.87 (x2) 2.27 (x7) 0.50 0.00 0
```

From 1067 to 1070 us it is 0.60, then 1.00. Iteration 21 has a clock of 0.93 there and takes 4.2 us more than in the change, with a stall of 1.97 us and a clock of 1.00.
